# A one-layer transformer on one core: q, k and v products in three fp32r passes, new instruction orders, h plus bias kept on chip

## The reference

```
h    = emb_weight[x] + 2 * (lora_A[:, x].T @ lora_B.T)                  # R = 16
xn   = layernorm(h)
q,k,v = split(xn @ Wqkv + bqkv)                                        # 256 -> 3 x 256
local  = softmax(q k^T / 4, |i - j| <= 64) v
global = softmax(q k[:64]^T / 4) v[:64]
gate = sigmoid(xn @ Wg + bg)
h    = h + ((1 - gate) * local + gate * global) @ Wout + bout
x2   = layernorm(h)
top 2 of 8 experts from softmax(x2 @ router_w.T), weights renormalised,
each expert takes at most 5121 of the 32768 pairs
h    = h + sum_k prob_k * (silu(x2 @ w1[e_k]) @ w2[e_k]) + x2
```

## Time and profile before

| | us |
|---|---|
| median of 3 runs | 3895.12 |
| profiled execution | 3882.32 |
| its span | 3880.6 |
| PE busy | 3481.5 (90%) |
| DVE busy | 2172.5 (56%) |
| ACT busy | 1868.3 (48%) |
| POOL busy | 2324.1 (60%) |

### The profile page before, as it was taken

One profiled execution on the slowest core, in us unless ns is written; L12 is line 12 of the kernel. 1 busy time (PEld: TensorE's weight loads), 2 busy tenths in 40 slices (PEclk: granted clock), 3 DMA queues, 4 the chain that ended last, 5 costly groups with the idle time before them and its releaser, 6 DMA issues. The chain is left out here.

```text
span 3880.6 us, 117579 instructions
## 1 busy us (share of the span) xinstructions
PE 3481.5 (90%) x47537; PEld 2753.0 (71%) x47537; DVE 2172.5 (56%) x5392; ACT 1868.3 (48%) x3086; POOL 2324.1 (60%) x2599
## 2 busy tenths in 40 slices
PE   2898889888888888888899849999999999999998
PEld 1555555555555555555555539999999999999998
DVE  3576767767676776767677634343434344443333
ACT  0455555555555555555555624343444444444343
POOL 5566777777777777777776645444544444444443
PEclk7899999999999999999999969999999999999999
DMA  4354544445454444545454323232323233222222
GB/s 142 123 157 117 163 122 151 130 138 139 128 152 123 150 133 135 144 125 149 124 154 130 109 87 65 50 68 46 71 48 72 48 69 72 46 51 45 45 45 41
DMA packets 242540, 398.31 MB, mean 103 GB/s; under 512 B 34572, under 2 KB 150748, under 8 KB 242044
## 3 DMA queue, kind: packets, MB, share of 16 engines
q1 hardware_dynamic: 168540, 297.43, 25.0%
q0 software_dynamic: 70512, 91.16, 13.8%
q10 hardware_dynamic: 3008, 2.95, 0.2%
HBM read 198.55 MB, written 192.88 MB: 101 GB/s over the span
## 5 line engine op out<-in xcount | busy, mean ns | idle before, releaser
L1388 POOL DMA_INDIRECT out_y<-out_t,tok_out x264 | 425.7, 1612 | 747.3 <-DMA out_y<-out_t,tok_out 405.0
L1534 ACT ACTIVATE act<-psS 128x512 f32<-128x512 f32 x528 | 316.9, 600 | 882.1 <-PE psS L1462 880.9
L1596 DVE TENSOR_TENSOR h_lo<-act,h_hi 128x512 fp32r<-128x512 f32 x528 | 367.2, 695 | 562.3 <-ACT h_hi L1535 543.8
L993 DVE TENSOR_REDUCE negm<-psS 128x4 f32<-128x640 f32 x512 | 418.8, 818 | 452.3 <-remote 276.3
L903 ACT ACTIVATE pl<-psS 128x896 f32<-128x896 f32 x512 | 467.7, 913 | 379.9 <-PE psS L741 372.0
L568 POOL TENSOR_SCALAR_AFFINE_SELECT pl<-pl 128x512 f32<-128x512 f32 x512 | 354.3, 692 | 448.4 <-ACT pl L903 446.2
L1497 PE MATMUL psO<-w_hi,h_hi 128*128 128x256 f32 x2112 | 598.8, 284 | 0.8 <-DVE h_lo L1596 0.8
L1497 PE MATMUL psO<-w_lo,h_hi 128*128 128x256 f32 x2112 | 588.7, 279 | 0.0
L1497 PE MATMUL psO<-w_hi,h_lo 128*128 128x256 f32 x2112 | 587.6, 278 | 0.0
L1462 PE MATMUL psS<-xg_hi,w_hi 128*128 128x256 f32 x1984 | 551.7, 278 | 0.0
L1462 PE MATMUL psS<-xg_hi,w_lo 128*128 128x256 f32 x1984 | 551.5, 278 | 0.0
(11 more groups left out here) (232 smaller groups left out, 7728.6 us busy)
## 6 DMA issues: line engine op xcount, KB each, us to landing
qk_scr<-qk SPq DMA_DIRECT2D x64, 768.0 KB
Q<-qk_scr SPq DMA_DIRECT2D x128, 384.0 KB
K<-qk_scr SPq DMA_DIRECT2D x128, 384.0 KB
qk_scr<-qk SPq DMA_DIRECT2D x64, 512.0 KB
qk_scr<-qk SPq DMA_DIRECT2D x64, 256.0 KB
h_rows<-held SPq DMA_DIRECT2D x32, 512.0 KB
hb<-h_rows SPq DMA_DIRECT2D x32, 512.0 KB
x_rows<-x SPq DMA_DIRECT2D x32, 512.0 KB
```

The lines of the kernel that those rows point to most:

```text
L993: dve.tensor_reduce(negm[:, g, 0, v, :, 2 * half:2 * half + 2], psS[:, 2:4, 0:2 * BAND].rearrange("p a (q u) -> p a q u", u=BAND), AX.X, A ...
L1388: pool.indirect_dma_start(out=y[:, :], in_=out_t[:, tile.out, s, :], in_offset=None, out_offset=bass.IndirectOffsetOnAxis(ap=tok_out[:, ti ...
L1534: act.activation(act32[:, b, :, 0:cols], src, ACT.Silu)
L1596: dve.tensor_tensor(h_lo[:, 2 * b:2 * b + 2, 0:cols], act32[:, b, :, 0:cols], h_hi[:, 2 * b:2 * b + 2, 0:cols].bitcast(F32), ALU.subtract) ...
```

## The change

1. The fp32 matmuls of q, k and v become fp32r matmuls on split operands. The first block cuts Wqk and Wv into a part in fp32r (wqk_hi, wv_hi) and the rest (wqk_lo, wv_lo). In the attention stage ACT writes xn_hi from PSUM and DVE, in a new step xn_lo, writes the rest (PSUM minus xn_hi). A product is then hi*hi + hi*lo + lo*hi: three fp32r matmuls for one fp32 matmul. The first 64 tokens are also written in front of the 512 (SIDE columns), so that one 128-wide slice holds them twice, and the global v is computed for all 256 output columns on 128 rows.
2. held becomes a ring of four sequences in SBUF (LIVE = 4). The DMAs to and from h_rows, the buffer hb and the tensor h_rows are gone; project adds held directly.
3. All five orders are new.

```
-            wv_sb / wqk (fp32)
+        wv_hi, wv_lo = keep(..., [P, KT, D], F32R)
+        wqk_hi, wqk_lo = keep(..., [P, KT, 4, P], F32R)
...
-            held = tmp("held", [P, QB, D])
-            hb = tmp("hb", [P, QB, D])
+            held = tmp("held", [P, LIVE, QB, D])
-            xn_t = tmp("xn_t", [P, KT, T])
+            xn_hi = tmp("xn_hi", [P, KT, SIDE + T], F32R)
+            xn_lo = tmp("xn_lo", [P, KT, SIDE + T], F32R)
...
 hold (POOL)
-                                need(pool, hold_out, 16 * s)
-                            pool.tensor_tensor(held[:, arg, :], h[:, arg, :], bout_b[:, :], ALU.add)
+                                need(pool, h1_done, 2 * (s - LIVE + 1))
+                            pool.tensor_tensor(held[:, s % LIVE, arg, :], h[:, arg, :], bout_b[:, :], ALU.add)
 SP
-                        if stage == "hb":
-                            sp.wait_ge(hold_out, 16 * (s + 1))
-                            need(sp, h1_done, 2 * s)
-                            sp.dma_start(hb[:, :, :], h_seq[s]).then_inc(hb_in, 16)
-                        if stage == "hold":
-                            sp.wait_ge(held_done, QB * (s + 1))
-                            sp.dma_start(h_seq[s], held[:, :, :]).then_inc(hold_out, 16)
 values, arg < 2 (PE)
-                                        last = pe.matmul(psX[:, b, j * D:(j + 1) * D], xn_t[:, k, tok], wv_sb[:, k, :],
-                                                         start=(k == 0), stop=(k == KT - 1))
+                                        for n, (x_, w) in enumerate(((xn_hi, wv_hi), (xn_hi, wv_lo), (xn_lo, wv_hi))):
+                                            last = pe.matmul(psX[:, b, j * D:(j + 1) * D], x_[:, k, tok], w[:, k, :],
+                                                             start=(k == 0 and n == 0), stop=(k == KT - 1 and n == 2))
 values, arg == 2 (PE)
-                                    for a in range(2):
-                                        last = pe.matmul(psX[64 * a:64 * (a + 1), b, 0:P], xn_t[:, k, 0:64], wv[:, k, a, :, :], ...)
+                                    for n, (x_, w) in enumerate(((xn_hi, wv_hi), (xn_hi, wv_lo), (xn_lo, wv_hi))):
+                                        last = pe.matmul(psX[:, b, 0:D], x_[:, k, 0:2 * SIDE], w[:, k, :], ...)
 qk (PE)
-                                last = pe.matmul(psX[:, b, :], wqk[:, k, arg, :], xn_t[:, k, :],
-                                                 start=(k == 0), stop=(k == KT - 1))
+                                for n, (w, x_) in enumerate(((wqk_hi, xn_hi), (wqk_hi, xn_lo), (wqk_lo, xn_hi))):
+                                    last = pe.matmul(psX[:, b, :], w[:, k, arg, :], x_[:, k, SIDE:SIDE + T],
+                                                     start=(k == 0 and n == 0), stop=(k == KT - 1 and n == 2))
 xn_t (ACT)
-                            act.activation(xn_t[:, arg, :], psX[:, b, :], ACT.Copy).then_inc(xn_t_done, 1)
+                            act.activation(xn_hi[:, arg, 0:SIDE], psX[:, b, 0:SIDE], ACT.Copy)
+                            act.activation(xn_hi[:, arg, SIDE:SIDE + T], psX[:, b, :], ACT.Copy).then_inc(xn_hi_done, 1)
 xn_lo (DVE), new
+                            dve.wait_ge(xn_hi_done, KT * s + arg + 1)
+                            x_ = psX[:, BANK["xn_t", arg, s], :]
+                            dve.tensor_tensor(xn_lo[:, arg, 0:SIDE], x_[:, 0:SIDE], xn_hi[:, arg, 0:SIDE].bitcast(F32), ALU.subtract)
+                            dve.tensor_tensor(xn_lo[:, arg, SIDE:SIDE + T], x_, xn_hi[:, arg, SIDE:SIDE + T].bitcast(F32),
+                                              ALU.subtract).then_inc(xn_lo_done, 1)
 project (DVE)
-                                dve.wait_ge(hb_in, 16 * (s + 1))
+                                dve.wait_ge(held_done, QB * (s + 1))
...
+                                              held[:, s % LIVE, 2 * arg:2 * arg + 2, :], ALU.add).then_inc(h1_done, 1)
...
 ORDER["pool"], one line of it
-                ("cur", "sel", 17), ("next", "gather", 0), ("far", "rstd1", None), ("cur", "sel", 18), ("next", "gather", 1),
-                ("past", "scatter", 2), ("next", "gather", 2), ("next", "gather", 3), ("past", "scatter", 3), ("next", "gather", 4),
+                ("far", "rstd1", None), ("cur", "sel", 18), ("next", "gather", 2), ("far", "hold", 0), ("next", "gather", 3),
+                ("far", "hold", 1),
```

More of the change, by code:

```diff
@@ L53 @@
 JOBS = 5 * QUARTERS
+LIVE = 4
 GROUPS = 3 * QUARTERS
@@ L139, in build @@
         la_t = keep("la_t", [P, T], F32R)
-        wqk = keep("wqk", [P, KT, 4, P])
+        wqk_hi = keep("wqk_hi", [P, KT, 4, P], F32R)
+        wqk_lo = keep("wqk_lo", [P, KT, 4, P], F32R)
         bqk = keep("bqk", [P, 4])
@@ L485, in build @@
-                ("nxt", "max", 19), ("nxt", "out", 2), ("nxt", "exp", 8), ("nxt", "out", 3), ("prev", "ahead", None),
-                ("cur", "attn_t", 0), ("far", "max", 0), ("cur", "attn_t", 1), ("nxt", "m_rows", 3), ("nxt", "exp", 9),
+                ("cur", "exp", 11), ("prev", "project", 1), ("nxt", "max", 3), ("cur", "out", 4), ("cur", "exp", 12),
+                ("far", "embed", None), ("nxt", "max", 4), ("cur", "exp", 13), ("cur", "out", 5), ("far", "lora", 0),
+                ("cur", "exp", 14), ("far", "lora", 1), ("nxt", "max", 5), ("cur", "out", 6), ("cur", "exp", 15), ("cur", "out", 7),
@@ new lines, in build @@
+                ("nxt", "max", 11), ("nxt", "exp", 1), ("far", "qk", 0), ("nxt", "max", 12), ("far", "qk", 1), ("nxt", "max", 13),
+                ("nxt", "exp", 2), ("far", "qk", 2), ("nxt", "max", 14), ("far", "qk", 3), ("nxt", "exp", 3), ("nxt", "max", 15),
+                ("cur", "mix", 0), ("nxt", "max", 16), ("nxt", "exp", 4), ("cur", "mix", 1), ("nxt", "out", 0), ("nxt", "max", 17),
+                ("nxt", "m_rows", 2), ("nxt", "exp", 5), ("cur", "mix", 2), ("nxt", "max", 18), ("nxt", "exp", 6),
@@ L487, in build @@
+                ("nxt", "out", 1), ("nxt", "max", 19), ("nxt", "exp", 7), ("cur", "mix", 3), ("nxt", "exp", 8), ("nxt", "out", 2),
+                ("nxt", "out", 3), ("nxt", "exp", 9), ("prev", "ahead", None), ("cur", "attn_t", 0), ("far", "max", 0),
+                ("cur", "attn_t", 1), ("nxt", "m_rows", 3), ("nxt", "exp", 10), ("far", "max", 1), ("cur", "project", 0),
+                ("far", "max", 2),
             )
             ORDER["act"] = (
-                ("cur", "exp", 11), ("cur", "evac", (1, 0)), ("cur", "exp", 12), ("far", "embed", None), ("cur", "exp", 13),
@@ L521, in build @@
+                ("past", "top", 6), ("far", "scale1", 3), ("nxt", "max", 10), ("far", "xn_lo", 0), ("far", "xn_lo", 1),
+                ("prev", "top", 0), ("nxt", "max", 11), ("prev", "top", 1), ("nxt", "max", 12),
             )
             ORDER["pool"] = (
-                ("nxt", "hold", 0), ("far", "gather", 5), ("cur", "sel", 0), ("cur", "sel", 1), ("nxt", "hold", 1),
-                ("nxt", "qk3", 0), ("nxt", "qk3", 1), ("nxt", "qk3", 2), ("nxt", "qk3", 3), ("cur", "sel", 2), ("prev", "mix", 0),
```

148 lines of the change are left out of this document (78 added, 70 removed).

## The result

The changed kernel takes **3738.2 us** (median, 3731.5 to 3747.4), the kernel before 3894.1 us beside it: a ratio of 0.9605, 95% interval 0.9577 to 0.9633. That is 156 us faster, and 73 us slower than the 3665 forecast. The profiled execution took 3731.5 us with a span of 3729.7.

A forecast was written before the change was run, and what follows sets the result against it. PE was taken as the bound, 89% busy in the attention stage. Period 59.7 - 2.7 + 0.75 - 0.2 + 0.8 + 1.0 = 59.4 us instead of 67.3 gave 3665 us; 8-in-10 range 3600 to 3790.

The forecast's parts named there:

- rival A: Attention stage: PE stays fed, clock 1.00, period 59.4 us; 3665 us, own range 3615 to 3715; chance 0.60.
- B: Four spaced gathers still thin PE out, clock falls once a period; period 63.4 us, 3782 us; chance 0.16.
- D: DVE takes over and PE waits at each of 20 max tiles, 3 us a period; 3752 us; chance 0.11.
- The burst: Six indirect DMAs in a row on POOL starve PE and lower its clock; being without them is worth 8.0 us a period.
- Rival C: POOL's new order returns nothing and only the products count; 3814 us; chance 0.08.
- What is given back: POOL's spaced DMAs: five lone gathers +0.75 us, parted pairs -0.2, four close gathers with holds +0.8 a period.
- ACT and DVE: xn_hi and xn_lo add work: 0.5 us for the first q product's wait, 0.5 for fuller DVE; bounds 0 and 3.
- the sum: Period 59.4 us; 29 periods -229 us, last two -3, first block +3; profiled 3653, timed 3665 with 12.8 offset kept.
- Products: Split q, k, v matmuls on PE take 9.1 us instead of 11.8: 2.7 us a sequence gained, bounds 0 and 5.5.
- Ring: Two DMAs of 0.5 MB a sequence go; no engine waits for them, so 0; bounds -0.3 and +2.
- Rival E: First quarter's load, behind the store of the maxima, comes late for PE's first max tile; 3910 us; chance 0.05.
- Around the loop: First block's weight cuts on DVE about +3 us; filling of the pipeline 0; expert stage 0.

The follow-up runs named there:

- e2: The kernel before with a 128x512 memset on POOL between any two neighbouring indirect DMAs, nothing else changed; 3695.5 us, ratio 0.9531.
- e12: e1 with six indirect DMAs standing next to each other on POOL again; 3870.4 us, ratio 0.9950.
- e1: The changed kernel with one DVE entry moved: la_cut 0 behind rank 0 and rank 1 instead of ahead of rank 0; 3647.9 us, ratio 0.9403.
- e9: e1 with fp32 products again instead of the split fp32r ones; 3720.0 us, ratio 0.9563.
- e3: The kernel before with the split products and the ring, its own orders kept (xn_lo behind max 11 on DVE); 3885.5 us, ratio 1.0008.
- e6: The kernel before with only the ring of four buffers in SBUF, store and load back removed; 3882.0 us, ratio 1.0003.
- e7: The kernel before with a short 128x16 memset on POOL between any two neighbouring indirect DMAs; 3880.9 us, ratio 1.0000.

## Why the prediction was right in its main part and 73 us too low

By its own sign the forecast, rival A, asked for a period of 59 to 60 us and a clock of 0.99. Neither came: they are 62.3 us and 0.97. A's own range ended at 3715, and 3738 lies in the stated one only because that had been drawn up to 3790 for B and D, of which neither is what happened: in that, it was luck. The profiled executions stand at 3731.5 against 3653, 78 us too low; 6 of them are hidden because the timed median stood 6.7 us above the profiled execution and not the 12.8 that I kept.

**The burst.** Right, and the trace gave its size: 8.0 us a period from one short period. e2, which changes nothing else, gains 6.2 us in the mean of its periods with 9 falls left; e12 loses 7.1. Rival C is refuted (3814; e2 alone is at 3695.5). The rule of the Trainium skill (SBUF — State Buffer, section "SBUF: two separate sides") that PE, ACT and DVE's own port pair never wait on anyone may hold for the port, and no run here tests it. What e2 and e12 show is that closely issued indirect DMAs cost these engines time all the same: in the earlier trace rows and in e12's 4.2 us they stand idle between instructions.

**What is given back.** I took 0.15 us for each gather that stands alone and 0.35 for the four with a hold between them, so +1.35 us. They cost at most 0.06 each, below my bound of 0 for the extra. Where the 0.15 had come from isn't shown; in e12 lone ones cost 0.07 each, although six stand together there again. In the changed kernel these four start about 2 us apart and the clock never falls at them, and e1 keeps them and has no fall in 28 periods. Rival B's mechanism is refuted at its place.

**The step that failed** is in "ACT and DVE" and "the sum": "I take 0.5 us for this, and 0.5 us for DVE being fuller", with none of DVE's moved steps priced by what it waits for. The order moves la_cut 0 ahead of rank 0, and on POOL the last gather that it needs was moved too. I weighed gathers by what they cost PE and not by when their rows land, though the trace before had DVE at the cast 6.2 us behind the last gather's issue. DVE waits 36.6 / 17 = 2.2 us for them, PE 1.9 behind it, and in 19 of 29 periods the clock falls: rival B's price, at a place that no rival named. The size is shown by e1: 79 us, where 73 were missing. By its ratio e1 would take 0.9403 x 3894 = 3662 us beside the kernel before; 3665 was written. That the two are so close is in part luck: the gathers cost less than I took and the waits for negm fell to 0.6 us a period instead of growing, and in their place stand waits that I didn't name, the longest 1.1 us for m_cut.

**Products.** 2.0 us a period net (e9) against 2.7 - 0.5; the matmuls themselves give 2.1 instead of 2.7, 0.6 short by the first matmul of each group, and the price that I set on xn_lo's wait wasn't due in the new orders: it isn't among PE's. It is due in the old ones (e3, 0.6 us a period).

**Ring.** 0, as forecast (e6, in the old orders).

**Rival D.** DVE is at 50.3 of 62.3 us, and PE's waits for negm, 37.8 us before, are below the list now. **Rival E.** The wait for K's load is 0.2 us in 17 sequences.

**Around the loop.** The gate of the first sequence comes 19.6 us later and the stretch behind the last gate is 17.9 us shorter, which belong together, since the gate stands elsewhere in the order; +1.7 us. The last two periods take 105.8 us instead of 112.1. Forecast: +3 and -3.

In sum for the profiled executions: 29 periods from 1950.9 to 1804.7 us, -146.2; -6.3; +1.7; together -150.8, which is the difference of the spans.

## What to carry to other kernels

Where engines run written-out orders, price each moved step by what it waits for and by what is queued behind it, also where the step itself is tiny: a 0.23 us cast cost 79 us. Look for a short or odd period in the trace before: it priced the burst at 8.0 us, and e2 and e12 gave 6.2 and 7.1. And where the clock falls, read gains as one thing with the falls: the same products are worth 62 us in the new orders and nothing in the old ones, where the clock is down for 79 us longer, and a wait of 1 us may be cheaper left alone.

## What the runs showed of the hardware

- Six indirect DMAs issued by POOL one behind the other go with idle stretches of microseconds on PE, ACT and DVE for which the trace names no producer, and their distance counts: starts 1.3 us apart cost 2.5 us of PE's time behind six (the kernel before), 1.5 us apart the same for six but 0.06 us each in a pair, 1.7 us or more apart at most 0.06 us each. An instruction between them that doesn't move the starts has no effect (e7).
- ACT can stand still for 4.2 us in such a burst though PE's last v product of that part had ended 0.5 us before it went idle (1044.8 and 1045.3 us in e12).
- Between the first and the last gate of these traces every stretch at 1.2 GHz lasted 3.4, 6.8 or 10.2 us.
- Split into three products, a matmul of 512 columns follows the one before after 0.23 us and one of 256 after 0.12; the first of each step takes 0.1 us more.
